# Graph network kernel on one Trainium2 core: the near group's rows leave PSUM in two copies of two chunks instead of one of four

## What is computed

```python
xc, xn = x[row], x[col]                      # row = src, col = dst
h = relu(xc @ W1[:d] + xn @ W1[d:] + b1)
mask = sigmoid(h @ W2 + b2)[:, 0]
agg = segment_sum(mask[:, None] * xn, row) / (segment_sum(mask, row)[row] + 1e-9)
out_emb = where(deg > 0, 0.5 * x + 0.5 * agg, x)
x = layernorm(x + relu(out_emb @ Wl + bl))
```

## Time and profile before

| | us |
|---|---|
| median of 3 runs | 4378.5 (4376.01 to 4381.13) |
| the profiled execution, device time | 4369.24 |
| its span in the profile | 4367.5 |
| the edge stage's near copies, first to last start | 2736.1 to 4271.9 |

### The profile page before, as it was taken

The page is one execution under the profiler, slowest core; times in us unless marked ns, Lnnn a source line. Parts: engine busy times, 40 slices in busy tenths (PEclk is TensorE's granted clock), DMA queues, the critical chain, the costliest instruction groups (busy, mean ns, idle before and its releaser), DMA issues. The chain is left out here.

```text
span 4367.5 us, 95747 instructions
## 1 busy us (share of the span) xinstructions
PE 3569.9 (82%) x20539; PEld 2439.5 (56%) x20540; DVE 3158.9 (72%) x12757; ACT 2150.9 (49%) x6722; POOL 1555.6 (36%) x1256
## 2 busy tenths in 40 slices
PE   4868882698888999986997996888888888888883
PEld 2367771333333444433444444777777778777783
DVE  8999987698888888873003005888888888888886
ACT  0078884266677888872003003444444444444444
POOL 0068874000000000001002002777777777777770
PEclk8855555799999999997998998999999999999996
DMA  2011113001111222224874882444444444444451
GB/s 47 1 10 15 15 17 81 10 34 51 68 68 77 95 93 103 94 86 187 303 276 165 304 297 85 144 137 141 138 138 142 136 141 138 137 138 140 141 134 40
DMA packets 276115, 498.31 MB, mean 114 GB/s; under 512 B 92068, under 2 KB 192571, under 8 KB 275883
## 3 DMA queue, kind: packets, MB, share of 16 engines
q1 hardware_dynamic: 209550, 347.01, 23.8%
q0 software_dynamic: 66336, 149.10, 12.4%
HBM read 391.18 MB, written 104.79 MB: 114 GB/s over the span
## 5 line engine op out<-in xcount | busy, mean ns | idle before, releaser
L1684 POOL DMA_INDIRECT xs<-edge_table,ea_row_stage x1088 | 1104.7, 1015 | 448.9 <-issue 432.7
L1868 PE MATMUL ea_psa<-xs,slot_dst 128*128 128x129 f32 x3264 | 458.5, 285 | 231.3 <-DVE agg_t L1782 231.2
L1868 PEld LDWEIGHTS ea_psa<-xs,slot_dst 128*128 128x128 f32 x3264 | 416.2, 195 | 264.3 <-DVE agg_t L1782 257.5
L1235 PE MATMUL a_agg_ps<-a_adj_ring,parts 128*128 128x512 f16 (+1 forms) x2548 | 523.6, 369 | 46.0 <-DMA a_adj_ring<-adjacency 45.9
L1902 ACT ACTIVATE slot_dst<-ea_onehot,ea_mask 128x128 f32<-128x128 f16 x1632 | 535.7, 399 | 13.2
L1782 DVE TENSOR_TENSOR agg_t<-agg_t,ea_psa 128x129 f32 x1632 | 460.5, 282 | 109.9 <-PE ea_psa L1868 97.5
L1034 PE MATMUL ab_agg_ps<-ab_adj_stage,parts 128*128 128x512 f16 x1911 | 529.6, 388 | 0.0
L1896 ACT ACTIVATE ea_mask<-ea_dot,b 128x4 f32<-128x4 f32 x408 | 121.3, 297 | 771.7 <-DVE slot_src L1807 771.7
L449 ACT ACTIVATE dst_step<-iota,dst_low_bias 128x128 f16<-128x128 f16 x1188 | 358.1, 401 | 216.0 <-PEq L474 213.0
L429 POOL DMA_INDIRECT records<-both_parts,record_row x98 | 348.5, 3556 | 314.8 <-ACT both_parts L455 291.8
L1375 POOL TENSOR_TENSOR parts<-xs,parts 128x896 f16<-128x896 f32 x7 | 13.2, 1881 | 1224.7 <-ACT parts L1369 1224.7
(11 more groups left out here) (379 smaller groups left out, 6463.6 us busy)
## 6 DMA issues: line engine op xcount, KB each, us to landing
a_adj_ring<-adjacency SPq DMA_DIRECT2D x182, 896.0 KB, 4.6
ea_low_rows<-low_rows SPq DMA_DIRECT2D x411, 128.0 KB
adjacency<-ab_adj_stage SPq DMA_DIRECT2D x91, 512.0 KB, 2.6
adjacency<-ab_adj_stage SPq DMA_DIRECT2D x91, 384.0 KB, 2.3
ea_near_rows<-near_rows SPq DMA_DIRECT2D x137, 128.0 KB
xs<-edge_table,ea_row_stage POOLq DMA_INDIRECT x1088
edge_table<-vx SPq DMA_DIRECT2D x12, 512.0 KB, 2.9
ea_row_stage<-row_columns SPq DMA_DIRECT2D x272, 2.0 KB
```

The costliest lines, as they stand in the source:

```text
L1235: ins = nc.tensor.matmul(ps[:, h, 0:width], lhs(r, t), ring[:, g % SLOTS, k * DB:k * DB + width], start=t == 0 and r == 0, stop=t == NT - ...
L1684: nc.gpsimd.indirect_dma_start(got[:, h, g, k, 0:ROW], None, m.table, bass.IndirectOffsetOnAxis(ap=row_s[:, h, g, k:k + 1], axis=0)).then_ ...
L1868: ins = nc.tensor.matmul(psa[:, home, k, 0:AW], hot_m[:, g, k, :], what, start=True, stop=True)
```

## The change

ScalarE's copy of part 1 of `psv` becomes two instructions, chunks 0 and 1 and then chunks 2 and 3, each of which adds one to `s_near_x`. VectorE's scores 0 and 1 wait for the first, scores 2 and 3 for the second. All waits on `s_near_x` count by two per turn. The sizes, the data and the order of the rest stay.

```diff
@@ vector, step
                     else:
                         adds[0]()
-                        dve.wait_ge(s_near_x, t + 1)
+                        dve.wait_ge(s_near_x, 2 * t + 1)
                     if seen >= 1:
                         dve.wait_ge(s_mask[g], t)
                     for k in range(G):
+                        if g == NEARBY and k == 2:
+                            dve.wait_ge(s_near_x, 2 * t + 2)
                         score = z[:, g, k, :] if g in FAR else psv[:, k, 0, :]
@@ tensor, lookups
                     if seen >= 1:
-                        pe.wait_ge(s_near_x, t)
+                        pe.wait_ge(s_near_x, 2 * t)
@@ scalar, step
-                        nc.scalar.activation(near_x[:, :, 0:D], psv[:, :, 1, :], ACT.Copy).then_inc(s_near_x, 1)
+                        for a in (0, 2):
+                            nc.scalar.activation(near_x[:, a:a + 2, 0:D], psv[:, a:a + 2, 1, :], ACT.Copy).then_inc(s_near_x, 1)
```

## The result

The changed kernel takes 4316.7 us (median of 4, 4313.7 to 4319.7), the kernel before beside it 4377.35. The ratio is 0.986, with a 95% interval of 0.984 to 0.988: 60.6 us less. The forecast was 4340.5 with a range of 4322 to 4358.

A forecast was written before the change was run, and what follows sets the result against it. The prediction took a chain passed between engines, with the copy wholly on it, as the bound. 0.19 us per turn directly, 0.28 with rarer clock falls, times 136 turns gave 38 us off 4378.5: 4340.5, range 4322 to 4358.

The forecast's parts named there:

- The chain: Edge stage turn: masks of group 1, copy, near scores, one-hots, last accumulation, next turn, with the copy wholly on it.
- The copy's term: Near-group copy cut in two: VectorE starts 0.19 us earlier per turn, 26 us in all, bounds 0 and 0.29 per turn.
- The second copy: On ScalarE: ends 0.10 us later than today's copy, hidden by idle time before the sigmoid, so costs nothing.
- the second wait: VectorE before score 2: second copy done at 0.67, score wants 1.05, so met with 0.38 us to spare.
- the counting by two: Wait values worked out in registers by VectorE's and TensorE's queues: taken as 0, bounds 0 and 0.12 us per turn.
- What a shorter turn does to the clock: TensorE's waits shrink to 2.16, 1.97, 1.53; a fall every second pair, 0.28 us less per turn, 38 us in all.
- the clock's share of the forecast: Part of the 0.28 us per turn beyond the copy's 0.19, from falls in every second pair instead of two in three.
- (b): TensorE's clock falls stop if a 1.97 us wait is too short: 10.84 per turn, 72 us less, 4306; chance 0.08.
- Case (a): Clock's share of slowed pairs stays two in three, leaving only the direct 26 us: 4352.5 us; chance 0.16.
- (c): Clock takes the gain back with a fall in each pair: 11.37 per turn, 4378 us, no change; chance 0.07.
- (d): (c) plus VectorE's queue late between near scores, eating 0.12 us: 11.49 per turn, 16 us more, 4394; chance 0.05.
- (e): Half copy costs nearly the whole, or PSUM readers take turns, so score 0 is no earlier: 4378 us; chance 0.04.

The follow-up runs named there:

- (1): Changed kernel with both copies, but VectorE waits for the second copy before score 0; 4380.9 us, ratio 1.0014 to the kernel before.
- (8): Changed kernel with ScalarE's two near copies put ahead of the mask products of group 1; 4277.4 us, ratio 0.9784 to the kernel before.
- the two filled kernels: TensorE does the four lookups of group 1 twice, in the kernel before (4335.2 us) and in the changed kernel (4306.7 us).
- the second trace: Second profiled execution of the changed kernel, nothing altered, with 21 clock falls; that set's median is 4313.8 us.
- the first trace: First profiled execution of the changed kernel, nothing altered, with 11 clock falls; that set's median is 4316.7 us.
- the doubled single lookup: Kernel before with one lookup of group 1 done twice by TensorE; 4372.5 us, ratio 0.9998, 41 falls.
- the kernel with the late accumulation (64 columns, h = 1): Changed kernel with a 64-column VectorE instruction ahead of the near group's last accumulation in every second turn; 4309.3 us, 13 falls.
- the uneven form: Changed kernel with a small VectorE instruction ahead of the near group's last accumulation in the h = 0 turns; 4333.0 us, 33 falls.

## Why the prediction was wrong, step by step

**The chain was read rightly.** Masks of group 1, copy, near scores, one-hots, last accumulation: taking back the early start (1) took back the gain, and moving the copy up the chain (8) brought 33 to 39 us more than the changed kernel (by the ratios 0.9784 and 0.9860, and by the medians 4277.4 and 4316.7).

**The copy's term was nearly right.** 0.19 per turn from the one row of 128x256, 26 us in all. Measured 0.20 from the undisturbed pairs and 0.21, 28.5 us, between the two filled kernels (26 by their ratios). A half takes 364 ns here, not 384. The budget of the Trainium skill, ScalarE: Activation LUTs, Rules for kernel authors, by its own difference 0.21 per turn, was as near, but its 0.51 for a half is not what the trace has. The page gives that budget for an ACTIVATE whose bias is a pointer operand, and these copies have no bias, which the prediction left out.

**The second copy, the second wait and the counting by two cost nothing that can be seen.** Score 2 never waits, the steps stay 0.21 apart (3386.71 to 3387.34 for three), the sigmoid still idles over 1.1 ahead of it, and the scores last 286 ns on average, as in the earlier trace rows. Score 0, the only one that runs beside a copy (the second), lasts 292 ns on average against 291 before. That agrees with the Trainium skill, PSUM — Partial Sum Buffer, Specifications (TRN2), on the two engines reading different banks.

**The step that failed is "What a shorter turn does to the clock".** It said that the waits become 2.16, 1.97 and 1.53, and from that a fall in every second pair, 0.28 per turn. The direction and the price of a fall (1.0 by the turns after, 22.65 for a slowed and a following turn against 21.66) held. The size did not: the clock's share of the forecast was 0.28 - 0.19 = 0.09 per turn, and it measured 0.45 - 0.20 = 0.25. The sentence that failed is that each wait shrinks by the same 0.19. Who ends the wait is VectorE's last accumulation, and in the turns h = 1 its place had slack that the trace before shows (the idle 0.54 at 3501.97) and the rows did not hold, and I did not use it. A one-hot stretched by 0.19 there moved the sums and shared the idle time out as 1.72 and 1.79, and after such waits the clock did not fall. Where the stretch was missing, the kernel came near to what was forecast, a fall every 44.4 us: in stretches of the second trace, and nearly throughout with the accumulation of the other turns made later (33 falls, after waits of 2.16). But even there the forecast had somewhat too many: after the waits of 1.90 to 2.10 the clock fell in 10 of 28 cases in the first trace and 18 of 45 in the second, where a fall in every second pair is one in two. Why the gathers lay so that 36 one-hots were stretched, and not 19 as in the second trace, is open, so how large this gain is in one execution is partly luck.

**The rivals.** The falls stop (b), 4306 us, was given 0.08 and is nearest to what happened; kernels whose waits are even or filled measure 4304 to 4310. Case (a), two in three, is what the doubled single lookup does to the kernel before, and the changed kernel does not do it. Nothing of (c), (d) or (e) was seen. The range left (b) out, because I held 1.97 for the typical wait and argued from its nearness to 2.16. The rows had a wait of 1.72 without a fall, so the distance from 1.97 to 1.72 was 0.25 us, and anything that moves one instruction by that much was able to decide. The condition of (b), that 1.97 is too short a wait, was itself wrong: 28 falls followed waits of 1.90 to 2.10 in the two traces of the changed kernel. The time came near (b) because such waits became fewer. The chance of 0.08 was too small for a term that hung on so little.

## What to carry to other kernels

Where two engines hand a turn back and forth, cut the copy between them so that the receiver starts on the first half (the halves lay in different banks here, and one bank was not tried), and price it with the nearest row of the same shape. Then ask what the shorter turn does to the idle times of the engine whose clock can fall. Their split between turns can matter more than their sum: an accumulation made 0.16 us later in one half of the turns gave 33 falls and 4333 us, and 0.20 us later in the other half no fall and 4304 us. An engine that idles before it falls may be given useless work: four lookups more per turn made the kernel before 38 us faster.

## What the runs showed of the hardware that was not expected

- VectorE's 128x512 one-hot from float16 takes up to 0.70 instead of 0.48 us where a gather's issue on GpSimd had begun about 0.5 us earlier (36 long ones in the changed kernel, 0.68 at the median), and not where it had begun 0.3 or 0.8 us earlier. All those over 0.51 us, 24 in the trace before and 36 in the one after, end 1.19 us after the gather's start, whether they began 0.49 or 0.64 us after it. Some that began 0.48 (three, before) or 0.64 to 0.68 us (one before, four after) behind a gather kept their 0.48, and there it is the gather that is long, 1.08 and 1.25 to 1.28 instead of 0.95 us. So one of the two gives way. Moving the gathers changed which ones are long. Which part of the gather's issue does this was not tried, and why the gathers keep one place for many turns and then slip to another stays open too.
- A single idle time of TensorE ahead of the sums was enough for its clock to fall from 2.4 to 1.2 GHz: 1.81 us in the kernel with the late accumulation (64 columns, h = 1). In the table it never fell after 1.80 us or less (860 cases), and after more than 2.1 us it stayed up in 73 of 172. What decides among equal waits stays open.
- Executions of one kernel differ by their falls: 11 and 21 in two profiled ones of the changed kernel, 4317.9 and 4329.7 us, and 4304.7 to 4342.4 us among six of the uneven form.
